# Layer 2 of a graph network: row gathers without the waits on TensorE's counting strips

## The reference

```
# x: 3125 x 128, 100000 edges (src, dst), sorted by dst, each with one of 8 types (rel)
h   = leaky_relu(gcn_conv(x, src, dst, W1, b1), 0.2)          # layer 0
out = gcn_conv(h, src, dst, W2, b2)                           # layer 1
x   = layernorm(x + out * sigmoid(ctx @ Wg + bg) + ctx @ Wb)

def rgcn_layer(x, W, SW, b):                                  # layers 2 and 3
    xt  = einsum('nd,rde->rne', x, W)      # a table of 8 rows for each node
    msg = xt[rel, src]                     # one row for each edge
    agg = segment_sum(msg, dst)
    return relu(agg + x @ SW + b)
x = layernorm(x + rgcn_layer(rgcn_layer(x, w1, sl1, b1), w2, sl2, b2))
```

## Time and profile before

| | |
|---|---|
| median of 3 runs | 1827.04 us (1826.1 to 1836.43) |
| the profiled execution | 1842.08 us, span 1840.2 us |
| granted TensorE clock, mean of the span | 0.949 of full speed |
| TensorE busy | 1562.5 us, 85% of the span |
| GpSimd busy | 917.4 us, 50% of the span |
| layer 2: first gather to last gather | 462.5 us to 1215 us |

### The profile page before, as it was taken

One profiled execution on the slowest core, in us unless ns is written; L12 is line 12 of the kernel. 1 busy time (PEld: TensorE's weight loads), 2 busy tenths in 40 slices (PEclk: granted clock), 3 DMA queues, 4 the chain that ended last, 5 costly groups with the idle time before them and its releaser, 6 DMA issues.

```text
span 1840.2 us, 25393 instructions
## 1 busy us (share of the span) xinstructions
PE 1562.5 (85%) x9744; PEld 949.8 (52%) x9744; DVE 779.7 (42%) x2390; ACT 520.8 (28%) x749; POOL 917.4 (50%) x931
## 2 busy tenths in 40 slices
PE   1379989998578889988899787898888998889986
PEld 1365554444355556555565455554555655556545
DVE  7999961337345555555465654530010010001102
ACT  0464520015234435444354543420000000000000
POOL 6500000000566566666666665646666666666665
PEclk9999999999789899999899998998999999989988
DMA  4312331534443444544455443325555355555441
GB/s 124 103 73 90 127 162 72 195 129 185 155 141 134 151 156 165 189 163 159 151 182 179 157 157 122 113 82 189 186 192 189 123 190 188 190 189 178 172 148 47
DMA packets 67473, 275.85 MB, mean 150 GB/s; under 512 B 19988, under 2 KB 25854, under 8 KB 54676
## 3 DMA queue, kind: packets, MB, share of 16 engines
q1 hardware_dynamic: 37940, 213.87, 30.1%
q0 software_dynamic: 29408, 60.29, 12.1%
HBM read 153.70 MB, written 120.38 MB: 149 GB/s over the span
## 4 chain that ended last, share of the span: by engine, by line
PE 66%; DVE 14%; another core or an unknown queue 6%; issue 6%; DMA 3%; POOL 2%; ACT 2%; POOLq 0%; DVEq 0%; ACTq 0%
PE ps L1385 34%; DVE hot_mem L1667 8%; PE ps L1408 8%; PE ps L1263 7%; PE ps L1297 7%; PE ps L1449 2%; PE ps L1435 2%; PE ps L1306 2%; ACT blocks L929 2%; DMA node_id<-table_rel,edges 1%; POOL node_id L798 1%; DMA acc<-table_rel,edges 1%; DVE hot_mem L1812 1%; POOL acc L798 1%
## 5 line engine op out<-in xcount | busy, mean ns | idle before, releaser
L798 POOL DMA_INDIRECT node_id<-table_rel,edges x445 | 439.0, 987 | 608.0 <-DMA table_rel<-node_id 358.3
L798 POOL DMA_INDIRECT acc<-table_rel,edges x429 | 419.3, 977 | 257.5 <-issue 113.2
L1385 PE MATMUL ps<-blocks,raw 128*128 128x512 f16 x1500 | 456.5, 393 | 15.5 <-DVE xn L1917 12.5
L929 ACT ACTIVATE blocks<-ps 128x800 f16<-128x800 f32 x384 | 315.6, 836 | 342.3 <-PE ps L1297 200.0
L1385 PE MATMUL ps<-blocks,dinv 128*128 128x512 f16 x1200 | 399.3, 395 | 13.5 <-issue 12.8
L1809 DVE TENSOR_SCALAR hot_mem<-cell_h,rel_cols 128x128 f16<-128x128 f16 x768 | 165.6, 268 | 265.9 <-PE ps L1297 152.9
L1297 PE MATMUL ps<-hot_mem 128*128 128x400 f16 x768 | 198.8, 344 | 68.0 <-ACT blocks L929 47.5
L1408 PEld LDWEIGHTS ps<-raw,node_id 128*128 128x128 f32 x996 | 193.8, 200 | 97.7 <-issue 38.9
L1385 PE MATMUL ps<-blocks,edges 128*128 128x512 f16 x600 | 236.8, 395 | 7.9 <-issue 7.6
L1408 PEld LDWEIGHTS ps<-raw,acc 128*128 128x128 f32 x962 | 183.7, 197 | 85.4 <-issue 31.0
L1812 DVE TENSOR_SCALAR hot_mem<-cell_h,rel_cols 128x400 f16<-128x400 f16 x768 | 224.8, 333 | 0.0
(11 more groups left out here) (183 smaller groups left out, 1296.2 us busy)
## 6 DMA issues: line engine op xcount, KB each, us to landing
rcounts<-blocks SPq DMA_DIRECT2D x44, 1600.0 KB
blocks<-rcounts SPq DMA_DIRECT2D x44, 1600.0 KB
counts<-blocks SPq DMA_DIRECT2D x6, 3200.0 KB, 11.0
blocks<-counts SPq DMA_DIRECT2D x5, 3200.0 KB, 10.5
table_rel<-node_id SPq DMA_DIRECT2D x50, 256.0 KB, 2.1
table_rel<-xn SPq DMA_DIRECT2D x50, 256.0 KB
node_id<-table_rel,edges POOLq DMA_INDIRECT x445
acc<-table_rel,edges POOLq DMA_INDIRECT x429
```

The source lines that it names most:

```text
L798: nc.gpsimd.indirect_dma_start(got[m % GATHERS][:, j, :], None, tables_rel[layer - 2], bass.IndirectOffsetOnAxis(ap=row_i[:, first + j:fir ...
L929: nc.scalar.activation(to.rearrange("p t (b m) -> p t b m", b=2), ps[:, strip_bank(k):strip_bank(k) + 2, 0:RCELLS].rearrange("p b (m t) -> ...
L1385: last = nc.tensor.matmul(ps[:, bank, 0:2 * HCOLS], part, half_pairs[u % 2][:, :, t * HCOLS:(t + 1) * HCOLS], start=(k == 0), stop=(k == T ...
```

## The change

The wait of layer 2's gathers on strips of slot n-2 is taken out, with the empty instruction behind it. The wait for a free buffer stays, and so does layer 3's wait.

```diff
                             first, chunks = gathers[layer].chunks(n)
                             for j in range(chunks):
-                                if layer == 2 and j % 2 == 0 and n >= AHEAD and made.steps[n - AHEAD]:
-                                    steps = made.steps[n - AHEAD]
-                                    pool.wait_ge(rstrip_counted, min(steps[0] + len(steps) * j // chunks + 1, MADE * HSTRIPS))
-                                    pool.nop(nofuse=True)
                                 if layer == 3 and j % 2 == 0 and n >= AHEAD and sums3[n - AHEAD]:
```

## The result

| | before | after |
|---|---|---|
| median in the same comparison | 1831.33 us (4 runs, 1826.1 to 1836.43) | 1936.08 us (4 runs, 1928.18 to 1943.1) |
| profiled execution, span | 1842.08, 1840.2 | 1928.18, 1926.4 |
| mean granted clock | 0.949 | 0.927 |

The ratio is 1.0571, with a 95% interval of 1.0514 to 1.0628: the change costs 105 us in the median. The forecast was +39, so the sign was right and the size was not. The experiments then showed that the loss isn't always there: where the kernel before takes 1625 us, which happened in four of the ten later comparisons, the changed kernel takes the same time (0.9991 of it, experiment 12).

The account below looks back on a forecast made before the run. It took layer 2 to be bound by TensorE's work plus 100.6 us of idle. Terms +17, +28, -15 and clock +9 gave +39 us on 1827, so 1866 us for the median, range 1803 to 1915.

Parts of the forecast that it names:

- What bounds the kernel, what the wait holds, what is late: Layer 2: TensorE's work plus 100.6 us idle; removed wait holds GpSimd 120.3 us; TensorE's signals late in long gather runs.
- the price of a long run: Unbroken gathers in layer 2: TensorE 50% busy once signals are late, from six stretches with 33.2 of 66 us.
- 64 - 48.95: TensorE's idle before the change in 482 to 546, 15.05 us, set against 32 us forecast, giving +17.
- at half rate: TensorE busy 50% while late signals last: 64 us gives 32 us idle at the start, 32 gives 16 per three-batch slot.
- the start: First gathers of layer 2: 64 go without a pause, to 544; +17 us, bounds +5 and +33.
- the triple slots: Around slots 18, 34 and 50 of layer 2: 32 unbroken gathers, +9 us each, +28 together, bounds +10 and +51.
- the gain of the other batches: The other 39 batches of layer 2, runs of 8 gathers then a pause: -15 us, bounds -29 and +20.
- Clock: TensorE loses clock when idle, 0.3 us for each us of idle: +9 us on 30, bounds -4 and +31.
- Rival D: Much slower: lateness grows with a run's length, the upper ends, 1827 + 90 to + 140; 8%.
- A, no change: Total of 469 gathers sets late signals whatever their order, or profiling mostly makes them: 1827 +- 18; 27% with C.
- B, faster: Gate causes catch-up runs of 10 to 18 gathers; cut to 8, ordinary batches cost 0.96 us each: 1804 us, 15%.
- C: The buffer wait would hold GpSimd as the removed wait did, so the change does nothing; 2%.

Follow-up runs that it names:

- experiment 12: The changed kernel itself, unaltered, rerun in the quiet condition: 1623.79 us beside 1624.74 for the kernel before, ratio 0.9991.
- experiment 6: Changed kernel with layer 2's gathers replaced by GpSimd clearing the buffer part and writing a scratch tile: 1734.08 us, late condition, ratio 0.9453 to the kernel before.
- experiment 8: Changed kernel with removed wait put back for batches 1 to 7, 22 to 25, 38 to 41, 54 to 57: 1966.96 us beside 1847.66, ratio 1.0591.
- experiment 9: Changed kernel with GpSimd waiting ahead of every eighth layer 2 gather until all have landed, late condition: 1846.52 us beside 1833.74, ratio 1.0065.
- experiment 4: Changed kernel with GpSimd waiting ahead of every eighth layer 2 gather until all have landed, quiet condition: 1773.97 us, ratio 1.0912 to the kernel before.

## Why the prediction was off

**What bounds the kernel, what the wait holds, what is late:** right for the condition of the first comparison. GpSimd was held by the removed wait, more than half of TensorE's 100.6 us of idle time was strips waiting for late copies (46.3 + 11.6), and without gathers (experiment 6) these waits nearly vanish. That long runs without a gap go with them holds in every late trace that I looked at, but it is not enough: in the quiet one a run of 469 does nothing. A second cause is needed, which no trace here shows.

**The step that failed is the price of a long run**, "64 - 48.95", "at half rate", in the start and in the triple slots. I took 50% from six stretches in runs of 11 to 24 gathers and carried it to runs of 48 and 32, as if lateness did not grow. It grows with the run: 7 us, 13, 23 in one run, so TensorE, with only two strips of lead, is busy 34% of the time at the start (23.01 of 67), and 58% around the first of the three-batch slots (29.70 of 51), where it had been 86% (26.51 of 31). **The start**: +17 forecast, +25.5 us of idle time measured (+28 with the slower matmuls), under the upper bound of 33. The run ended at 48 gathers, not 64, as slot 0 was not summed in time, which saved nothing, since it was TensorE that was slow. **The triple slots**: +28 forecast, +44 of idle time measured (+55 with the slower matmuls, the upper bound being 51), though each run was 24 gathers and not 32.

**A second step failed, the gain of the other batches**: -15 forecast, +6 of idle time measured (+8 with the matmuls). The runs of 8 that I expected did form, 27 in all, and by themselves they cost little: in 807 to 869, 1018 to 1053 and 1097 to 1132, which hold 11 of them and no other run, TensorE idles 132 - 118.07 = 13.9 us, 1.3 for each, against 0.96 in the forecast and 1.7 in the mean before. What I had wrong is that nothing else would form. A late signal also delays the sum that frees the next buffer, two buffers then come free close together, and GpSimd goes through 15 or 16 gathers (seven such runs, five of them between 552 and 890). That the delayed sum joins the runs is my reading of the trace; no run tests it. **Clock**: +9 forecast, +15 measured in layer 2. The forecast was small because its idle time was, 30 us against 76; for each us of idle the clock cost 0.2 us, less than the 0.3 taken. The sum is 91 in place of 39; of the 52 missing us, 25 are the price of the long runs, 21 the other batches and 6 the clock.

Rival D, lateness that grows with a run's length, was the true one: 1936 lies in its 1917 to 1967. I gave it 8%, though rows 6 had 6.8 and 6.2 us of wait within 24 gathers and no row at all had a run of 48. The range of 1803 to 1915 left most of it out. The sign of the change came out right for the reason given, the bunching; the size did not.

**The other rivals.** A, no change, fell in the late condition. In the quiet one its number is right, but not its reasons: there no signal is late at all. The Trainium skill, SBUF — State Buffer, "Who interferes with whom", which has DMA and compute engines not contend, agrees with the quiet runs; in the late ones TensorE still stood still beside the gathers, though halving their bytes changed nothing (1.0510, against 1.0500 to 1.0571). So the amount of data isn't what delays the signals; whether anything contends for a port or a path, no trace here shows. B, faster, was right that runs of 8 with such pauses keep the lateness small (3.9 us at most), and wrong that all ordinary batches would run so and that start and slots would stay at their lower ends. C fell with GpSimd's waits.

**What I had asked of the profile:** 56 or more gathers in a row from 462, there were 48; no gather held by a strip, right; idle of TensorE in 482 to 546 near 32, it was 64 - 25.94 = 38; in layer 2 near 130, it was 827 - 649.72 = 177 (475 to 1302); runs of 32 around the three-batch slots, 24; "remote" well over 93, 180.6; GpSimd busy the same, 905.5 and 917.4. Of the two signs of being wrong neither came: TensorE was busy 34% in the long first run, not above 80%, and of the runs of 8 only one, which began 0.46 us behind another, had a late copy at its first gather.

## What to carry to other kernels

If an engine's releases come late in a trace ("remote" ahead of an engine whose producer was long done), look how long the neighbouring queue of indirect gathers had been running without a gap: a wait that seems only to hold gathers back may be what leaves gaps, and taking it out, wholly or in part, joins short runs to long ones. Price such a run by its length, not by the mean share of shorter ones, and ask of every wait put back what is released at once behind it. And compare kernels only beside each other: the same program took 1625 and 1850 us on the same chip, and a change worth 5% in one condition was worth nothing in the other.

## What the runs showed of the hardware

- Two conditions of a chip, with the kernel before at 1625 or at 1829 to 1853 us. Gathers are issued as quickly in both (0.94 us each, 0.30 apart). In the quiet traces "remote" stands nowhere. Layer 3, which the change doesn't touch, is longer too: from its first gather to the end of the span 1620.6 - 1097.45 = 523 us quiet and 1926.4 - 1318.26 = 608 us late, both in the changed kernel. What sets the condition is open.
- In the late condition signals from TensorE reach ScalarE, VectorE and GpSimd late while gathers are issued without a gap. ScalarE waits up to 23.0 us for them in the changed kernel and 26.5 in experiment 8, VectorE up to 22.9 and GpSimd up to 7.5 in the changed kernel. The last late signal of the longest runs comes through 3.8 us (changed kernel) or 3.7 to 6.7 us (experiment 8) behind the run's last gather. Signals from ScalarE to TensorE are on time in the same stretch, 0.9 us from a copy's start to the next strip. The path that is held up was only argued from these waits; it was not seen.
- Runs of 8 gathers with gaps of 2.3 us, in which all gathers land, hold the waits to 3.5 us (experiment 9). Runs of 8 with gaps from 1.6 us, without a wait for landing, hold them to 3.9 us (changed kernel).
- Gaps of 2.3 us for the landing of 8 gathers are the same in both conditions (experiment 4, quiet, and 9, late): the landings reach GpSimd as quickly in either.
